# Two gated attention-and-expert layers: four normalised row tiles get buffers of their own, the top-2 choice is split six and two, the token list comes from cumulative flags, and TensorE gets filler matmuls

## The reference

```python
x = x + jnp.tanh(g_xattn[0]) * _L0_xattn_ref(_layernorm(x, axis=-1), ctx_4096, ctx_4096, mask_1x1xSxS2_bk0, ...)
x = x + jnp.tanh(g_ffn[0]) * _L0_ffn_ref(_layernorm(x, axis=-1), ...)
x = x + jnp.tanh(g_xattn[1]) * _L1_xattn_ref(_layernorm(x, axis=-1), ctx_4096, mask_Bx1x4096_ff1, ...)
x = x + jnp.tanh(g_ffn[1]) * _L1_ffn_ref(_layernorm(x, axis=-1), ...)
```

```python
TOP_K = 2
logits = x @ W_gate + b_gate
_, top_idx = jax.lax.top_k(logits, TOP_K)
y_all = jax.nn.relu(jnp.einsum('bsd,edh->bseh', x, W_e) + b_e)
y = jnp.take_along_axis(y_all, top_idx[..., None], axis=2)
return y.mean(axis=2)
```

## Time and profile before

| what | value |
|---|---|
| median of 3 runs | 933.17 us (932.38 to 933.29) |
| the profiled execution, its own time | 933.38 us |
| its span in the trace | 931.6 us |
| PE busy | 867.4 us, 93% of the span |
| DVE busy | 603.6 us, 65% |
| ACT, POOL busy | 326.5 us, 415.6 us |
| mean granted TensorE clock | 0.974 |

### The profile page before, as it was taken

The page is one execution under the profiler, slowest core; times in us unless marked ns, Lnnn a source line. Parts: engine busy times, 40 slices in busy tenths (PEclk is TensorE's granted clock), DMA queues, the critical chain, the costliest instruction groups (busy, mean ns, idle before and its releaser), DMA issues.

```text
span 931.6 us, 13834 instructions
## 1 busy us (share of the span) xinstructions
PE 867.4 (93%) x4747; PEld 707.1 (76%) x4747; DVE 603.6 (65%) x1061; ACT 326.5 (35%) x590; POOL 415.6 (45%) x423
## 2 busy tenths in 40 slices
PE   5999999999999999999999999998899998849992
PEld 4777878977877787877897887776699996437881
DVE  5975675276576446476537567668898886676445
ACT  4423133214114204214222313322266677443230
POOL 4652352163163243163225233324888775527651
PEclk9999999999999999999999999999899999959997
DMA  9020130011111002012002002030344320843547
GB/s 321 16 91 1 34 91 1 12 46 46 34 53 38 14 1 91 1 45 80 1 12 90 1 1 80 2 114 20 84 130 124 82 55 26 307 168 113 175 166 289
DMA packets 42321, 71.17 MB, mean 76 GB/s; under 512 B 7050, under 2 KB 14795, under 8 KB 42067
## 3 DMA queue, kind: packets, MB, share of 16 engines
q1 hardware_dynamic: 37138, 58.00, 19.4%
q0 software_dynamic: 3680, 12.06, 3.9%
q10 hardware_dynamic: 1440, 0.24, 0.1%
HBM read 53.64 MB, written 10.22 MB: 69 GB/s over the span
## 4 chain that ended last, share of the span: by engine, by line
PE 85%; DVE 6%; issue 2%; DMA 2%; POOL 2%; ACT 2%; ACTq 1%; SPq 0%; DVEq 0%
PE ps L1412 18%; PE ps L1414 18%; PE ps L1413 18%; PE ps L1533 6%; PE ps L1525 6%; PE ps L1662 5%; PE ps L1541 3%; PE ps L1650 3%; PE ps L1643 2%; PE ps L1773 1%; DVE h L954 1%; PE ps L1618 1%; PE ps L1633 1%; DMA y_in<-y_rows 1%; PE ps L1728 1%
## 5 line engine op out<-in xcount | busy, mean ns | idle before, releaser
L544 POOL TENSOR_TENSOR q_t<-rot_a,rot_b 128x512 f32<-128x512 f32 x64 | 82.7, 1293 | 151.2 <-DVE rot_b L999 151.2
L997 DVE TENSOR_TENSOR rot_a<-ps,cos 128x512 f32<-128x512 f32 x80 | 55.2, 690 | 85.9 <-PE ps L1414 85.2
L1412 PE MATMUL ps<-xt_hi,wq_hi 128*128 128x512 f32 x256 | 107.6, 420 | 0.5 <-DVE rot_b L999 0.5
L1412 PE MATMUL ps<-wo_hi,at_hi 128*128 128x512 f32 x256 | 106.7, 417 | 0.4 <-DVE at_lo L1105 0.4
L1414 PE MATMUL ps<-xt_hi,wq_lo 128*128 128x512 f32 x256 | 101.1, 395 | 0.0
L1413 PE MATMUL ps<-xt_lo,wq_hi 128*128 128x512 f32 x256 | 101.0, 394 | 0.0
L1414 PE MATMUL ps<-wo_hi,at_lo 128*128 128x512 f32 x256 | 100.2, 391 | 0.0
L779 ACT ACTIVATE ps<-ps 128x512 f32<-128x512 f32 x64 | 37.2, 581 | 178.6 <-PE ps L1525 178.6
L1413 PE MATMUL ps<-wo_lo,at_hi 128*128 128x512 f32 x256 | 99.8, 390 | 0.0
L792 ACT ACTIVATE at_hi<-ps 128x512 fp32r<-128x512 f32 x64 | 38.3, 598 | 171.6 <-PE ps L1541 171.6
L1110 DVE TENSOR_TENSOR X<-ps,X 128x512 f32<-128x512 f32 x64 | 44.2, 691 | 73.9 <-PE ps L1414 73.6
(11 more groups left out here) (223 smaller groups left out, 2083.9 us busy)
## 6 DMA issues: line engine op xcount, KB each, us to landing
wq_raw<-in_wq SPq DMA_DIRECT2D x8, 1024.0 KB, 5.5
wo_raw<-in_wo SPq DMA_DIRECT2D x8, 1024.0 KB, 5.3
w_raw<-in_we SPq DMA_DIRECT2D x8, 1024.0 KB, 6.7
X<-in_x SPq DMA_DIRECT2D x4, 512.0 KB, 12.5
wk_raw<-in_wk SPq DMA_DIRECT2D x8, 256.0 KB, 2.9
q_t<-in_ctx_t SPq DMA_DIRECT2D x2, 1024.0 KB, 9.8
wv_raw<-in_wv SPq DMA_DIRECT2D x4, 512.0 KB, 4.4
ctx_s<-in_ctx SPq DMA_DIRECT2D x8, 256.0 KB, 2.9
```

The lines of the kernel that those rows point to most:

```text
L544: nc.gpsimd.tensor_tensor(dst, rot_a[:, r % 2, :], rot_b[:, r % 2, :], ALU.add).then_inc(rope_ok, 1)
L997: nc.vector.tensor_tensor(heads(rot_a[:, r % 2, :]), heads(bank), bcast(cos[:, :], 4), ALU.mult)
L1412: nc.tensor.matmul(dst, w_hi, x_hi, start=start and k == 0, stop=False)
```

## The change

Four things change, all between the last attention batch and the first expert.

**Buffers.** A new tile set `h3` holds the normalised rows of batches 4 to 7, so each of the eight batches has its own place (`final_row(b)`), and the waits before batches 4 to 7 go. `h3` lies where `be_b` is loaded later, so SP now waits for all copies of the rows to DRAM before that load. `h_rows` gets one row more in front, filled by a small copy, for padding entries to point at.

**Choice.** `choose(0)` now takes six batches (EARLY) and `choose(1)` two. PE sums the mask batch by batch into eight counts, six of the eight matmuls before the second `choose` is waited for.

**List.** The reduction `n_e` goes. The flags `reached` stay cumulative: DVE no longer subtracts neighbours over 384 elements, but multiplies them as they are, and subtracts once in the 24 columns that come back. `tile_hot` stands before `slot_lo`. The small chain to `gather_i` is written anew.

**Fillers.** `keep_warm(n)` is n matmuls of 512 columns in fp32 whose result nobody reads: two behind the early sums, five behind the running counts, four behind the list matmuls.

```diff
+        h3 = sb("h3", [P, 4, D])
...
-        h_rows = nc.dram_tensor("h_rows", (N, D), F32).ap()
+        h_rows = nc.dram_tensor("h_rows", (1 + N, D), F32).ap()
...
+        EARLY = 6
...
+        def final_row(b):
+            return h[:, b, :] if b < 2 else h2[:, b - 2, :] if b < 4 else h3[:, b - 4, :]
...
-                sp.dma_start(h_rows[b * P:(b + 1) * P, :], (h if b % 4 < 2 else h2)[:, b % 2, :]).then_inc(hrow_out, 16)
+                sp.dma_start(h_rows[1 + b * P:1 + (b + 1) * P, :], final_row(b)).then_inc(hrow_out, 16)
...
+            sp.dma_start(h_rows[0:1, :], x[0, 0:1, :]).then_inc(hrow_out, 16)
...
             sp.wait_ge(gate_mm, CREDIT + B)
+            sp.wait_ge(hrow_out, 16 * (B + 1))
             sp.dma_start(be_b[:, :, :], be.unsqueeze(0).to_broadcast([P, EX, D])).then_inc(be_in, 16)
...
             def final_rows(b, j):
                 ve.wait_ge(rstd_ok, CREDIT + B * 3 + b + 1)
-                if b >= 4:
-                    ve.wait_ge(ht_mm, CREDIT + 2 * B + b - 3)
-                    ve.wait_ge(hrow_out, 16 * 4)
-                normalise(b, j, h_ok, h if b % 4 < 2 else h2)
+                nc.vector.tensor_scalar(final_row(b), X[:, b, :], mean[:, b:b + 1], rstd[:, b:b + 1],
+                                        ALU.subtract, ALU.mult).then_inc(h_ok, 1)
...
-                at = slice(4 * half, 4 * half + 4)
+                at = slice(EARLY, B) if half else slice(0, EARLY)
+                n = at.stop - at.start
...
-                ve.wait_ge(gate_mm, CREDIT + 4 * half + 4)
+                ve.wait_ge(gate_mm, CREDIT + at.stop)
...
+            def keep_warm(n):
+                for _ in range(n):
+                    nc.tensor.matmul(ps[:, 5, :], ident[:, :], X[:, 0, :], start=True, stop=True)
+
+            def chosen(b):
+                return nc.tensor.matmul(ps[:, 0, 0:EX], ones_r[:, :], sel[:, b, :], start=b == 0, stop=b == B - 1)
+
             pe.wait_ge(kz_ok, CREDIT + 1)
             pe.wait_ge(tri_ok, CREDIT + 1)
+            pe.wait_ge(sel_ok, CREDIT + 1)
+            for b in range(EARLY):
+                chosen(b)
+            keep_warm(2)
             pe.wait_ge(sel_ok, CREDIT + 2)
-            nc.tensor.matmul(ps[:, 0, 0:64], ones_r[:, :], sel[:, :, :], start=True, stop=True).then_inc(rank_mm, 1)
+            for b in range(EARLY, B):
+                last = chosen(b)
+            last.then_inc(rank_mm, 1)
...
+            keep_warm(5)
...
+            keep_warm(4)
             turn_in(0)
```

More of the change, by code:

```diff
@@ L237, in flamingo_gated_two_layers @@
         be_b = sb("be_b", [P, EX, D])
+        assert place[0] <= at_xt + 8 * KT * N
+        place[0] = at_xt + 4 * KT * N
+        h3 = sb("h3", [P, 4, D])
         assert place[0] <= at_xt + 8 * KT * N
@@ L1341, in _ @@
                                         ALU.is_equal).then_inc(hot_ok, 1)
+            at = slice(0, NT)
             ve.wait_ge(list_mm, CREDIT + 1)
-            nc.vector.tensor_scalar(second[:, :], ps[:, 3, 128:128 + NC], N + 0.5, -float(N), ALU.is_gt, ALU.mult).then_inc(slot_ok, 1)
-            nc.vector.tensor_scalar(padding[:, :], ps[:, 3, 128:128 + NC], 0.5, None, ALU.is_lt).then_inc(slot_ok, 1)
-            nc.vector.tensor_scalar(listed[:, :], ps[:, 3, 128:128 + NC], -1.0, None, ALU.add).then_inc(slot_ok, 1)
@@ L1347, in _ @@
-            ve.wait_ge(slot_ok, CREDIT + 17)
-            nc.vector.tensor_tensor(row_of[:, :], listed[:, :], second[:, :], ALU.add).then_inc(slot_ok, 1)
-            ve.wait_ge(slot_ok, CREDIT + 18)
-            nc.vector.tensor_scalar(gather_i[:, :], row_of[:, :], 0.0, None, ALU.max).then_inc(slot_ok, 1)
-            nc.vector.tensor_tensor(padding[:, :], padding[:, :], spare, ALU.mult).then_inc(slot_ok, 1)
+            nc.vector.tensor_copy(upto[:, :], ps[:, 3, 128:128 + NC]).then_inc(slot_ok, 1)
@@ new lines, in _ @@
+            ve.wait_ge(slot_ok, CREDIT + 13)
+            nc.vector.tensor_tensor(listed[:, at], upto[:, 0:NT], upto[:, 1:NC], ALU.subtract).then_inc(slot_ok, 1)
+            ve.wait_ge(slot_ok, CREDIT + 14)
+            nc.vector.tensor_scalar(second[:, at], listed[:, at], N + 0.5, -float(N), ALU.is_gt, ALU.mult).then_inc(slot_ok, 1)
+            nc.vector.scalar_tensor_tensor(padding[:, at], listed[:, at], 0.5, spare[:, at], ALU.is_lt, ALU.mult).then_inc(slot_ok, 1)
+            ve.wait_ge(slot_ok, CREDIT + 15)
@@ L1352, in _ @@
+            nc.vector.tensor_tensor(gather_i[:, at], second[:, at], listed[:, at], ALU.add).then_inc(slot_ok, 1)
+            ve.wait_ge(slot_ok, CREDIT + 16)
+            nc.vector.scalar_tensor_tensor(scatter_i[:, at], listed[:, at], -1.0, padding[:, at], ALU.add, ALU.add).then_inc(slot_ok, 1)
             nc.vector.tensor_tensor(t_upto[:, :], t_before[:, :], t_e[:, :], ALU.add).then_inc(slot_ok, 1)
+            passed = rank_a[:, 2:5, :, :].rearrange("p b e f -> p (b e) f")
+            ve.wait_ge(slot_ok, CREDIT + 19)
@@ L1358, in _ @@
-            ve.wait_ge(slot_ok, CREDIT + 23)
-            nc.vector.tensor_reduce(of_tile[:, :], passed, AX.X, ALU.add).then_inc(slot_ok, 1)
-            ve.wait_ge(slot_ok, CREDIT + 24)
             nc.vector.tensor_scalar(of_tile_i[:, :], of_tile[:, :], EX - 1.0, None, ALU.min).then_inc(slot_ok, 1)
@@ L1717, in turn_last @@
             def turn_last(b):
-                rows = h if b % 4 < 2 else h2
                 pe.wait_ge(h_ok, CREDIT + 2 * B + b + 1)
@@ L1721, in turn_last @@
                 for k in range(KT):
-                    last = nc.tensor.transpose(ps[:, b % 2, k * P:(k + 1) * P], rows[:, b % 2, k * P:(k + 1) * P], ident[:, :])
+                    last = nc.tensor.transpose(ps[:, b % 2, k * P:(k + 1) * P], final_row(b)[:, k * P:(k + 1) * P], ident[:, :])
                 last.then_inc(ht_mm, 1)
```

69 lines of the change are left out of this document (33 added, 36 removed).

## The result

| | before | changed |
|---|---|---|
| median of 20 runs | 933.80 us (932.38 to 936.86) | 931.36 us (927.49 to 946.7) |
| ratio | 1 | 0.9969, 95% interval 0.9955 to 0.9982 |
| profiled execution, its own time | 933.38 us | 927.49 us |
| its span | 931.6 us | 925.7 us |

The ratio leaves out the one disturbed run of 946.7. The median fell by 2.4 us, not by 5.6. The profiled execution of the changed kernel is the fastest of its 20, and its total came out almost as forecast. So one profile hides the result: the question is what the other executions do.

What follows compares the result with a forecast made beforehand. TensorE was taken to bound the kernel, so only its idle stretches could shrink. Shifts of 3.6, less 0.9, then 1.7 and 3.2 after the list, plus 2.4, made 5.6 us off 933.38: 927.8, range 926.5 to 929.0 (chance 0.52).

Steps and rivals of the forecast that it cites:

- Part one, the buffers: Attention rows of batches 4 to 7: without DVE's buffer wait the last gate columns come 3.6 us earlier.
- Part two, the choice: Splitting `choose` six and two ends the second `sel` at 815.0; the split loses 0.9 us, leaving a shift of 2.7.
- Parts three and four: Sums with two fillers, then the list: counts start at 816.4, shift 1.7; list matmuls end at 824.0, shift 3.2.
- Part five: Gather and first expert tile: product starts 0.6 us sooner behind the first turn and saves 1.8 at full clock; together 2.4.
- I take the full clock here: First two fillers: PE keeps full clock through its 1.7 us rest, so fillers take 0.94 us each, not 1.78.
- the first rival: Clock lost at the first fillers or first two turns, 1.7 us each: 929.5 for one, 931.2 for both; chance 0.26.
- The slower rival: Fillers run at 1.2 GHz without raising the clock, 1.78 us each, and become the bound: 939 us; chance 0.05.
- The experts took the early start: Rival at the seventh expert: POOL's chain or row arrival decides, part five's 2.4 us are lost: 930.2; chance 0.10.
- Nothing in stage one was late: Rival: DVE's chain or ACT late elsewhere in stage one, the buffers give perhaps 1.5 us: 931.7 to 933.4; chance 0.07.

Runs made afterwards that it cites:

- b1_buffers_only: The kernel before with only the new row buffers and SP's wait before the bias load; 930.40 us, 0.9972 of before.
- k3: The kernel before, unaltered, profiled again; that execution took 934.44 us.
- d1_early4: The changed kernel with the choice split four and four instead of six and two, fillers kept; 927.74 us, 0.9933 of before.
- i3: The changed kernel, unaltered, profiled again; that execution took 934.11 us.
- o4_changed_look: The changed kernel, unaltered, profiled again; that execution took 931.32 us.
- a1_again: The changed kernel, unaltered, measured again; median 929.79 us, 0.9958 of before; its profiled execution took 932.11 us.

## Why the prediction was wrong

**Part one, the buffers: right, its size a little high.** Forecast 3.6 us at the last gate columns, 3.9 between the first profiles of both kernels (31.4 to 27.5), 2.9 in the median of b1_buffers_only. Two things that the profiles show lower it: k3 did not have the wait, and b1 lost 0.7 us behind the gate columns. The instants came as forecast: batches 5 and 7 at 804.1 and 805.5 (forecast 804.3 and 805.7), gate columns ending at 811.45 (811.55). The new wait of SP cost nothing visible: the bias load was issued at 811.48 and took 9.8 us, and DVE first added the bias at 835.08.

**Part two, the choice: right.** The second `sel` ended at 814.73; forecast 815.0. Against four and four it loses 0.8 us (forecast 0.9): the second `sel` ends 3.51 us behind the start of the last gate columns here and 2.72 in d1_early4. At the start of the counts it is 1.2, which also counts the fillers that no longer stand in the way; without fillers it can't be seen in the medians.

**Parts three and four, in an execution that keeps the clock there: right, the gain forecast too low.** Counts at 816.0 (forecast 816.4), one-hot rows at 819.85 (820.3), list matmuls 820.69 to 823.0 (to 824.0), since five fillers took 4.0 us and not 4.7. The shift at the end of the list was 4.2, not 3.2.

**Part five: half of it came.** It was to add 2.4 and added 1.1. The product was to start 2.1 us behind the first turn and started 2.60 behind it (2.68 before); that is no matter of the clock, since in i3, with both turns at full clock, it was 2.71. And it was to run at full clock, saving 1.8, but the clock was at 0.50 until about 833.0, and it saved 0.8. So the first tile ended 5.3 us earlier where 5.6 was forecast because 1.0 us too little in one part met 1.3 too much in the other: that the sum fits the first profile is partly luck. The span fell by 5.9; the other 0.6 came behind the seventh expert and wasn't followed.

**The step that failed is "I take the full clock here" in part three, with the price of the first rival.** I reasoned from the earlier trace rows that PE could rest 1.7 us and keep the clock, and gave its loss at either place 0.26. It was lost before the fillers' end in 3 of 6 profiled executions of this kernel, around the first two turns in 4 of 6, and in every one at one of the two places at least. I priced a loss at either place at 1.7 us, half clock over 3.5 us of work, taking from the earlier trace rows that the clock is back after that. At the turns that was enough, 0.9 to 2.1 us. At the first place it stayed at 0.50 for 7 to 10 us, and since sums, fillers and list stand in one line on PE with DVE waiting between them, the list came 3.3 to 4.9 us late. That is more than fillers and list changes had gained: gate columns to third turn is 23.5 us in one kind of execution and 27.6 to 28.1 in the other, against 25.1 before. The mean of that stretch over the six (25.7) is no better than before, so what remains in the median is part one; b1_buffers_only, with part one alone, has nearly the same ratio, 0.9972. Six profiles are few for the share of each kind.

The slower rival had this mechanism, fillers at 1.78 us each, and I gave it 0.05 because I took it for all or nothing. It happens in part, and often. The measured 931.36 lies where the first rival put the clock lost at both places, 931.2, but not for its reason: only one of the six profiles lost it at both.

**The other rivals.** The experts took the early start in full: POOL's chain moved by 5.3 us, and the stop at the seventh expert stayed 1.5 us. Nothing in stage one was late in the six profiles.

The median of the changed kernel over all its 36 executions here is 930.9 us; 9 of the 36 are below 929, the upper end of the forecast. So the range I forecast is reached by one execution in four.

## What to carry to other kernels

A filler matmul that stands ahead of needed work on TensorE must be priced at its half-clock duration too (here 1.78 us, not 0.94): in the executions in which the clock had already fallen, the fillers were in the way. Put fillers where the engine waits for something that is surely later than they end even at that price, as in the four and four split, where they run beside the second `choose`.

One profile of a kernel whose runs spread over 9 us is one draw: take several, measure between marks inside the kernel, and count how many fall into each kind before explaining a median. Compare each term of a sum with its own measurement, since errors of two terms can cancel in the total. A wait seen in one profile (here 2.94 us) may also be absent in the next.

## What was not expected of the hardware

The granted clock stayed at 0.50 through 9.5 us in which PE has no idle time between its records (the ends of matmuls are modelled, so that says nothing of how full the array was). The windows of PE in o4_changed_look and in a1_again:

```profile
814.80:824.30 9.50, 9.50 (x24) 0.50 0.69 256
```

```profile
815.80:821.80 6.00, 6.00 (x16) 0.50 0.62 253
```

In both the stretch holds small sums (8 to 64 columns) and fp32 fillers of 512 columns. The stretch at 0.50 in the earlier trace rows, also without a gap, is 3.0 us long, and the clock was back by 808.8. So being busy is not enough to foretell when the clock returns, and equal code of the same kernel kept it under the fillers in three executions and lost it in three.
